# A graph kernel's last phase: three slots of a block picked by TensorE, 22 copied by GpSimd, the third pick ahead of the add-up

## The reference

```python
h = node_feats_in @ Wn.T + bn          # 12500 x 64, the table hn
h_src = h[src]                         # one row of 64 for each edge
w = ssp(edge_feats @ We1.T + be1)      # ssp(x) = softplus(x) - log 2
w = ssp(w @ We2.T + be2)
m = h_src * w
agg = segment_sum(m, dst)              # sum over the edges of a destination
```

## Time and profile before

| | |
|---|---|
| median of 3 runs | 8763.74 us |
| the profiled execution | 8762.05 us |
| its span, first to last instruction | 8760.1 us |
| share of the span with TensorE busy | 87% |
| TensorE weight loads | 79% |
| GpSimd | 71% |
| ScalarE | 67% |
| VectorE | 63% |
| mean granted TensorE clock | 0.951 of full speed |

### The profile page before, as it was taken

The page is one execution under the profiler, slowest core; times in us unless marked ns, Lnnn a source line. Parts: engine busy times, 40 slices in busy tenths (PEclk is TensorE's granted clock), DMA queues, the critical chain, the costliest instruction groups (busy, mean ns, idle before and its releaser), DMA issues. The chain is left out here.

```text
span 8760.1 us, 165117 instructions
## 1 busy us (share of the span) xinstructions
PE 7637.1 (87%) x51516; PEld 6905.6 (79%) x51517; DVE 5505.1 (63%) x7447; ACT 5860.1 (67%) x10176; POOL 6259.5 (71%) x6471
## 2 busy tenths in 40 slices
PE   7999999999989999999999777777777777888887
PEld 6999999888889999998888666666666666776775
DVE  5655656666645555556666666666666666777777
ACT  5777777666657777776666566666666666666665
POOL 5777777766557777777664477777777777777776
PEclk9999999999989999999999798988988889999999
DMA  2111112111111111111111222222222222222222
GB/s 75 35 34 35 35 34 35 31 30 28 25 40 34 35 34 35 34 34 31 31 30 23 75 56 59 55 57 57 55 58 56 55 59 55 55 59 56 55 56 59
DMA packets 341135, 392.62 MB, mean 45 GB/s; under 512 B 165119, under 2 KB 240563, under 8 KB 340564
## 3 DMA queue, kind: packets, MB, share of 16 engines
q0 software_dynamic: 204000, 151.96, 12.1%
q1 hardware_dynamic: 136750, 239.87, 8.1%
q10 hardware_dynamic: 322, 0.03, 0.0%
HBM read 375.47 MB, written 15.92 MB: 45 GB/s over the span
## 5 line engine op out<-in xcount | busy, mean ns | idle before, releaser
L699 PE MATMUL banks<-split_sb,e_low_hot 128*128 128x400 f32 x22000 | 4092.6, 346 | 45.6 <-DVE split_sb L752 45.6
L699 PEld LDWEIGHTS banks<-split_sb,e_low_hot 128*128 128x128 f32 x22000 | 4015.6, 189 | 74.1 <-DVE split_sb L752 46.1
L922 POOL DMA_INDIRECT big<-hn_table,src_i x2875 | 2857.0, 994 | 883.7 <-issue 870.7
L645 POOL DMA_INDIRECT big<-p_table,src_i x1750 | 1655.8, 946 | 695.2 <-issue 528.7
L758 DVE TENSOR_REDUCE picked<-banks 128x48 f32<-128x1200 f32 x1000 | 1300.1, 1300 | 1352.1 <-PE banks L699 1351.1
L670 ACT ACTIVATE e_low_hot<-e_key_off 128x1536 fp32r<-128x1536 f16 x1000 | 1381.1, 1381 | 1130.6 <-PE banks L699 1112.7
L645 POOL DMA_INDIRECT big<-h_table,src_i x1750 | 1674.9, 957 | 612.5 <-issue 529.6
L666 ACT ACTIVATE e_key_off<-e_key_in,node_off 128x384 f16<-128x384 f16 (+1 forms) x4000 | 2028.4, 577 | 125.5 <-DMA e_key_in<-sel_dram 41.4
L957 PE MATMUL banks<-hn_split,e_low_hot 128*128 128x448 f32 x7000 | 1500.1, 370 | 75.5 <-issue 70.1
L957 PEld LDWEIGHTS banks<-hn_split,e_low_hot 128*128 128x128 f32 x7000 | 1298.0, 188 | 217.1 <-issue 96.6
L781 DVE TENSOR_TENSOR hot<-e_dst_pair,banks 128x1536 bf16<-128x1536 bf16 (+1 forms) x934 | 931.1, 997 | 69.9 <-issue 0.6
(11 more groups left out here) (216 smaller groups left out, 4491.7 us busy)
## 6 DMA issues: line engine op xcount, KB each, us to landing
e_wide<-in_edge_t SPq DMA_DIRECT2D x125, 832.0 KB
e_key_in<-sel_dram SPq DMA_DIRECT2D x250, 343.8 KB
big<-hn_table,src_i POOLq DMA_INDIRECT x2875
big<-p_table,src_i POOLq DMA_INDIRECT x1750
big<-h_table,src_i POOLq DMA_INDIRECT x1750
e_key_in<-gate_dram SPq DMA_DIRECT2D x125, 64.0 KB
src_i<-in_src SPq DMA_DIRECT2D x375, 12.5 KB, 1.7
e_key_in<-sel_dram SPq DMA_DIRECT2D x250, 8.2 KB
```

The costliest lines, as they stand in the source:

```text
L645: pool.indirect_dma_start(buf[u][:, j, 0:ROW0], None, table, bass.IndirectOffsetOnAxis(ap=src_i[u][:, j:j + 1], axis=0),).then_inc(gathere ...
L699: last = pe.matmul(o, low_hot[gr][:, h, e], split_sb[:, part, h * HI1:(h + 1) * HI1, :], start=(h == 0 and part == 0), stop=(h == HI2 - 1 ...
L922: pool.indirect_dma_start(buf[u][:, j, 0:F], None, table, bass.IndirectOffsetOnAxis(ap=src_i[u][:, j:j + 1], axis=0),).then_inc(gathered[u ...
```

## The change

`GSEL` goes from 2 to 3. So `took` goes from 23 to 22: GpSimd issues one indirect DMA less per block, and the keys, `low_hot`, `high` and the first-phase key arithmetic get one slot more. TensorE has `pick(n+1, 2)` between `first_layer(n+2)` and `add_up(n)`. ScalarE has a third `low_hots` behind the second. VectorE has `take(n+1, 2)` right behind `take(n+1, 1)`, between `make_hot(0)` and the visits. Two scratch tiles move into the space of `h1_degT`, which is not in use in this phase, and `gate_q_i` gets a place of its own.

```diff
-GSEL = 2
+GSEL = 3
...
-            high = tiles.enter_context(nc.sbuf_tensor(f"{tag}_high", [P, GSEL, GHIGH], F32))
-            masked = tiles.enter_context(nc.sbuf_tensor(f"{tag}_masked", [P, F, GHIGH], F32))
+            masked = h1_degT[:, 0:F * GHIGH].rearrange("p (f a) -> p f a", a=GHIGH)
+            high = h1_degT[:, F * GHIGH:(F + GSEL) * GHIGH].rearrange("p (s a) -> p s a", a=GHIGH)
...
                         pick(n + 1, 1)
                         if not isinstance(n, int) or n + 2 < NB:
                             first_layer(n + 2, turn_of(g, u) + 1, u % 2)
+                        pick(n + 1, 2)
                         add_up(n, g, u)
...
                     pick(0, 1)
+                    pick(0, 2)
...
-                            low_hots(n + 2, 1, turn_of(g, u) + 1, u % 2)
+                            for s in range(1, GSEL):
+                                low_hots(n + 2, s, turn_of(g, u) + 1, u % 2)
...
                         if values_ahead:
                             take(n + 1, 1, (u + 1) % 2)
+                            take(n + 1, 2, (u + 1) % 2)
                         with dve.Fori(since, to) as visit:
```

More of the change, by code:

```diff
@@ L193, in gnn_kernel @@
         acc = sb("acc", [P, ACC])
-        h1_degT = sb("h1_degT", [CQ * (H + 1), NPACK * P])
+        h1_degT = sb("h1_degT", [P, NPACK * P])
         inv_deg = sb("inv_deg", [P, NQ])
@@ L277, in gnn_kernel @@
         gate_row = tiles.enter_context(nc.sbuf_tensor("gate_row", [NB, GSEL * P], F16))
-        gate_src_i, gate_p_i, gate_q_i = [
+        gate_q_i = tiles.enter_context(nc.sbuf_tensor("gate_q_i", [P, 2, GSEL * P], I32))
+        gate_src_i, gate_p_i = [
             h1_deg[:, :, :].rearrange("p n c -> p (n c)")[:, k * 2 * GSEL * P:(k + 1) * 2 * GSEL * P]
-            .bitcast(I32).rearrange("p (s c) -> p s c", s=2) for k in range(3)]
+            .bitcast(I32).rearrange("p (s c) -> p s c", s=2) for k in range(2)]
         digit_i = tiles.enter_context(nc.sbuf_tensor("digit_i", [P, DIGITS, HI2, 32], I32))
@@ L932, in _, with first_layer @@
                     pe.sem_inc(hot_used[1], 1)
-                    def first_layer(n, turn, u):
+                    def first_layer(n, turn, u, groups=range(NG)):
                         pe.wait_ge(e_in[u], 16 * turn)
-                        for q in range(NG):
+                        for q in groups:
                             cs, w = cols_of(q)
@@ L1051, in _ @@
                     second_logs(0)
-                    low_hots(0, 1, 1, 0)
+                    for s in range(1, GSEL):
+                        low_hots(0, s, 1, 0)
                     first_logs(1)
-                    low_hots(1, 0, 1, 1)
-                    low_hots(1, 1, 1, 1)
+                    for s in range(GSEL):
+                        low_hots(1, s, 1, 1)
                     with act.Fori(0, turns) as g:
@@ L1165, in _ @@
                     gates(0)
-                    take(0, 0, 0)
-                    take(0, 1, 0)
+                    for s in range(GSEL):
+                        take(0, s, 0)
                     first_activation(1)
@@ L1248, in _ @@
                     w = min(4, NPACK - k) * P
-                    act.copy(h1_degT[:, k * P:k * P + w], bank[4 + k // 4][0:CQ * (H + 1), 0:w])
+                    act.copy(h1_degT[0:CQ * (H + 1), k * P:k * P + w], bank[4 + k // 4][0:CQ * (H + 1), 0:w])
             @block.gpsimd
@@ L1340, in _ @@
                         pe.wait_ge(c_scaled, k - 2)
-                    pe.matmul(o[:, 0:CQ * F], h1_degT[:, k * P:(k + 1) * P], w2_diag[:, :], start=True, stop=False)
+                    pe.matmul(o[:, 0:CQ * F], h1_degT[0:CQ * (H + 1), k * P:(k + 1) * P], w2_diag[:, :], start=True, stop=False)
                     for i in range(CQ):
```

## The result

The changed kernel takes 9030.5 us (median of 4 runs, 9026.91 to 9041.59) against 8763.7 us: 1.0304 times the kernel before, with an interval of 1.0292 to 1.0316. It is slower by 267 us. The prediction was 8936 us with a range of 8850 to 9000: the right side, but 94 us too little and outside the range.

A forecast was written before the change was run, and what follows sets the result against it. GpSimd's copies were taken to bound the kernel, then the TensorE–VectorE chain: 79 x 29.6 and 44 x 34.0 us put the last product 171.1 us later, plus 1.3 us of key arithmetic, so 8936 us, range 8850 to 9000.

The forecast's parts named there:

- GpSimd bounds the kernel before, and its saved copy alone is worth up to 162 us: Gate phase: GpSimd's 23 copies of 1.296 us set the pace; one less saves 125 x 1.296 = 162 us.
- The chain takes over from GpSimd: One-visit blocks: the chain through TensorE and VectorE takes 29.6 us, above GpSimd's 28.5, so the wait for copies vanishes.
- the signs named: Profile after: GpSimd waits for TensorE, product for no copy, mask some 5 us; idleness 2.3, first layer 3.0, spacing 29.6 and 34.0.
- Two visits cost 4.27 us more: Two-visit blocks: first make_hot(1) to the pick takes 8.43 us in place of 4.16, 4.27 more, giving 33.9 us.
- 34.0 us in all: Two-visit blocks: 29.6 + 4.27 = 33.9 us, with 0.1 us for the clock taken as 34.0 us a block.
- The clock term: TensorE idles some 2.3 us between add-up halves; 0.1 us a block taken, between nothing and 1.1 us.
- rival (c): Between add-up halves: 2.3 us of idleness lowers the clock, 0.6 us more in each block, 9010 us; 11 in 100.
- The start: Ahead of the loop: pick(1, 0) starts at 4992.3, first_layer(2) comes at 5006.8 and the first third pick at 5009.7.
- Rival (a): Gate phase: GpSimd stays the bound, TensorE's weight loads leaving room for a third pick, 8602 us; 4 in 100.
- Rival (b): Gate phase: chain tighter than added up, 28.6 us with one visit, 33.0 with two, full clock, 8804 us; 8 in 100.

The follow-up runs named there:

- e4_b22: The kernel before with 22 copies in place of 23 and no third pick, slot 22 counting as zero: 8609.32 us, ratio 0.9821.
- e5_fill4: The changed kernel with four extra matmuls, result not used, between the third pick and the add-up on TensorE: 8897.2 us, ratio 1.0153.
- e3_copy23: The changed kernel with GpSimd copying 23 slots as before, the third pick's result going to a spare place: 9029.59 us, ratio 1.0301.
- e2_late: The changed kernel with take(n+1, 2) on VectorE behind the visits in place of ahead of them: 8937.48 us, ratio 1.0198.
- e7_split: e2_late with groups 2 and 3 of the first layer moved behind the add-up on TensorE: 8796.88 us, ratio 1.0036.
- e6_fill_else: The changed kernel with nine extra matmuls, result not used, ahead of the third pick on TensorE: 9252.96 us, ratio 1.0556.

## Why the prediction was right and wrong

- **GpSimd bounds the kernel before, and its saved copy alone is worth up to 162 us**: right; e4_b22 gave 154.
- **The chain takes over from GpSimd**: right. In the quick block shown every link came within 0.15 us, and none longer than forecast: first to second pick 8.57 (forecast 8.67), second pick to first layer 5.76 (5.87), first layer 2.71 (2.8), pick to mask 5.95 (6.05), mask to `make_hot(1)` 2.18 (2.25), `make_hot(1)` to pick 3.75 (3.75 in that loop half). With the clock held up, e5_fill4 shows 29.0 and 29.5 by turns, mean 29.3, where the sum was 29.6. Of the signs named, the product's and GpSimd's waits, the mask's wait (4.9 us), the idleness (2.4) and the first layer (2.95) came true; the one-visit spacing of 30.7 lies outside the 29.0 to 30.3 given for it.
- **Two visits cost 4.27 us more**: right, 4.27 in e5_fill4 (33.58 and 29.31). **34.0 us in all**: 34.1 measured, but partly by luck. With the clock held up it is 33.6; the sum without the clock term (33.9) was 0.3 us too long, and that term 0.5 too small.
- **The clock term**: this is the step that failed. The prediction took 0.1 us a block for the 2.3 us of idleness in two-visit blocks, 44 x 0.1 = 4 us in all, and the 29.6 us of a one-visit block hold nothing for it, without a reason given. Measured, with the gap filled in part and everything else the same (e5_fill4), the clock is worth 9030.5 - 8897.2 = 133 us, 1.1 us a block. The other terms were some 35 us too long, so that 94 us of miss are left. The mechanism was rival (c), which I had priced at 0.6 us a block (9010 us) and given 11 in 100: its place and its direction were right, its size about half of what it is.
- **Why the price was too small**: I took it from one quick and one slow half 1 and looked at half 1 alone, 1.1 us at the most. Two things were in the trace of the kernel before. First, how often: in its two-visit stage half 1 was slow behind 21 of the 39 gaps of 2.4 to 2.5 us that the timeline shows, 0.4 us a gap on average. Second, what stands behind half 1. There it is another visit, and of the 89 picks counted in that stage none took over 6.03 us. Behind the slow half 1 at 8009.88 come:

```profile
8013.16 1.91 PE L974 MATMUL banks<-hot,big 128*64 128x128 f32 x26 [0.67 <-DVE acc L1153]
8015.24 1.53 PE L974 MATMUL banks<-hot,big 128*64 128x128 f32 x24 [0.17 <-DVE hot L1116]
8017.53 5.90 PE L957 MATMUL banks<-hn_split,e_low_hot 128*128 128x448 f32 x28 [0.76 <-issue]
```

In a one-visit block the pick follows at once, and it lost 1.80 us more in the block shown. That a drop can cost more than 1.1 us stood in the earlier trace rows too: the first layer took 4.96 us there in place of 2.96. (The prediction calls that half the clock; granted over that stretch was 0.61.)

- **The one-visit blocks** before had no gap above 1.8 us between the halves and no slow half 1. Their granted clock of 0.90 goes with the idleness of 5.1 to 5.3 us ahead of the first layer, which took 4.5 to 5.9 us behind it in place of 2.96; there the chain had 8.9 us of reserve. The changed kernel is slower at a higher mean clock (0.967 against 0.951): what counts is where the clock falls.
- **The start**: the first third pick came at 5006.37, not 5009.7, 3 us early. Of the 46 two-visit blocks one is block 78, not 79, which changes no sum. From the product of the last block to the end it is 72.4 us, 71.4 before.
- **Rival (a)** fell. GpSimd waits for TensorE, and e3_copy23 gave it a copy more for nothing. The Trainium skill (Perfetto Trace Analysis, Identifying the Most-Contended Engine) says to judge TensorE's headroom by the share of weight loads. That share is 1717.93 / 2200 = 78% in the changed kernel's one-visit stage, while the chain through TensorE sets every block's time, so the 22% that it leaves could not be used in this order. The take between pick and visits was a part of the matter, as e2_late shows, and the clock another.
- **Rival (b)**, 8804 us with 28.6 and 33.0 us a block: not for the change, but e7_split, with the same work in another order, came to 28.6 and 32.7 and to 8797 us.

Left open: why the clock falls in about every second one-visit block of the changed kernel and less often in e6_fill_else, behind the same idleness. I made no run that varies the spacing alone.

## What to carry to other kernels

Work that is moved from a bound engine to one with room has to be placed, not only counted: between a producer and the consumer that the next stage waits for, a pick of 6 us and its 2.3 us of masking came in full, where behind the visits and with the waiting filled the same work hid in the one-visit blocks. When a chain loses its reserve, price every drop of the clock on it for as long as the clock stays low, with the work that will stand behind it in the new order, and count in the trace how often it comes. See also whether work that has to be done anyway can lie in the gap. And where blocks differ (one visit or two here), decide the change for each kind: it gained 1.3 us a block in one and lost 2.8 in the other even in its better order.

## What the runs showed of the hardware

- Nine matmuls whose result nobody reads (2.17 us a block) made the kernel 131 us faster, four (1.05 us) did the same: 8899 and 8897 us against 9030.
- Behind 1.52 us of idleness half 1 ran in 1.53 us each time (78 of 78 in e5_fill4's one-visit stage). Behind 2.40 and 2.41 us it took between 1.53 and 2.83 us, slow in 42 of 75 cases in the changed kernel's one-visit stage, and the pick behind it took up to 8.1 us in place of 5.9.
- How often it was slow behind the same 2.41 us differed: 42 of 75 and 18 of 48 in the two stages of the changed kernel, 23 of 72 and 39 of 51 with nine matmuls more ahead of the third pick (e6_fill_else).
